# A new start and new step orders for a gated linear kernel with Strassen-type products on one Trainium2 core

## What is computed

```python
xn = (x - mean(x)) / sqrt(var(x) + 1e-5)          # x: 2 x 1024 rows of 1024, by row
w  = weight * (32x32 block of the mask has any 1) # 1024 x 1024
s  = xn @ w.T + bias
base  = xn @ W_org.T
q     = mean over the 1024 rows of a batch of xn, @ Wq.T
coeffs = softmax(q @ lora_keys.T / sqrt(128))     # 8 experts, one set per batch
delta = sum over e of coeffs[e] * (xn @ lora_down[e]) @ lora_up[e]
out = x + s * silu(base + delta)
```

## Time and profile before

| | |
|---|---|
| runs | 438.54, 437.90, 437.91 us; median 437.91 us |
| profiled execution: span from first to last instruction | 438.5 us (beside the slowest of the three runs, 438.54) |
| PE busy | 424.7 us, 97% |
| DVE busy | 334.7 us, 76% |
| ACT busy | 216.4 us, 49% |
| POOL busy | 104.9 us, 24% |
| chain that ended last | PE 75%, DMA 14%, DVE 4%, POOL 2% |
| mean DMA rate | 230 GB/s |

### The profile page before, as it was taken

How to read it: one execution, slowest core, us unless ns; L and a number is a source line. 1 busy time by engine, 2 the same in 40 slices (tenths; PEclk the granted TensorE clock), 3 DMA queues, 4 the chain that set the end, 5 groups by cost and what they waited for, 6 DMA issues and landing times.

```text
span 438.5 us, 5903 instructions
## 1 busy us (share of the span) xinstructions
PE 424.7 (97%) x1910; PEld 345.7 (79%) x1910; DVE 334.7 (76%) x492; ACT 216.4 (49%) x379; POOL 104.9 (24%) x91
## 2 busy tenths in 40 slices
...
GB/s 299 413 416 240 161 266 255 280 210 218 195 237 264 265 290 283 290 325 362 179 73 144 49 114 275 287 236 336 410 386 165 96 76 21 72 270 242 265 160 96
DMA packets 40862, 101.05 MB, mean 230 GB/s; under 512 B 4608, under 2 KB 4864, under 8 KB 40064
## 3 DMA queue, kind: packets, MB, share of 16 engines
...
...
HBM read 71.31 MB, written 29.36 MB: 230 GB/s over the span
## 4 chain that ended last, share of the span: by engine, by line
PE 75%; DMA 14%; DVE 4%; POOL 2%; SPq 2%; issue 1%; ACT 1%; DVEq 0%; ACTq 0%; POOLq 0%
PE psA L864 24%; PE psA L866 24%; PE psA L865 24%; DMA x_nat_sb<-in_x_nat_dram 4%; DMA d_dram<-d_split 3%; DMA a_raw<-in_up_dram 2%; DMA out_dram<-cst 2%; DMA worg_sb<-in_w_org_dram 2%; DMA b_hi<-d_dram 2%; PE psA L883 1%; DVE nat_stats L1154 1%; DMA temp<-in_down_dram 1%; SPq L796 1%; DVE cst L1323 1%; POOL x_nat_sb L1365 1%
## 5 line engine op out<-in xcount | busy, mean ns | idle before, releaser
L864 PE MATMUL psA<-b_hi,a_hi 128*128 128x512 f32 (+1 forms) x444 | 173.6, 391 | 0.5 <-ACT snaps L1107 0.5
L866 PE MATMUL psA<-b_hi,a_lo 128*128 128x512 f32 (+1 forms) x444 | 172.1, 388 | 0.0
L865 PE MATMUL psA<-b_lo,a_hi 128*128 128x512 f32 (+1 forms) x444 | 172.0, 387 | 0.0
L864 PEld LDWEIGHTS psA<-b_hi,a_hi 128*128 128x128 f32 x444 | 83.4, 188 | 18.4 <-ACT snaps L1107 0.9
L866 PEld LDWEIGHTS psA<-b_hi,a_lo 128*128 128x128 f32 x444 | 83.4, 188 | 17.1
L865 PEld LDWEIGHTS psA<-b_lo,a_hi 128*128 128x128 f32 x444 | 83.4, 188 | 16.6
L1078 ACT ACTIVATE b_hi<-b_raw 128x512 fp32r<-128x512 f32 (+2 forms) x66 | 45.3, 716 | 56.0 <-DVE b_raw L1232 36.5
L1219 DVE TENSOR_TENSOR b_lo<-b_raw,b_hi 128x512 fp32r<-128x512 f32 (+2 forms) x66 | 52.0, 814 | 8.6 <-ACT b_hi L1078 8.3
L1395 POOL TENSOR_TENSOR cst<-cst,xres 128x512 f32<-128x512 f32 x15 | 23.0, 1534 | 98.7 <-DVE cst L1323 98.7
L1107 ACT ACTIVATE snaps<-psA 128x512 f32<-128x512 f32 x39 | 23.2, 595 | 42.8 <-PE psA L866 42.6
L1219 DVE TENSOR_TENSOR a_lo<-s_raw,a_hi 128x512 fp32r<-128x512 f32 x52 | 37.4, 733 | 5.2 <-ACT a_hi L1068 5.2
...
## 6 DMA issues: line engine op xcount, KB each, us to landing
...
```

The lines of the kernel that those rows point to most:

```text
L864: nc.tensor.matmul(ps, l_hi, r_hi, start=first, stop=False, skip_group_check=True)
L865: nc.tensor.matmul(ps, l_hi, r_lo, start=False, stop=False, skip_group_check=True)
L866: return nc.tensor.matmul(ps, l_lo, r_hi, start=False, stop=over, skip_group_check=True)
```

## The change

The identity is made first on POOL and has a semaphore of its own (`pool_ident`), for which the warm-up on PE and the first reduction on DVE wait; before, they waited for all constants. The first `CP` waits for the table `sel`, and `G` for `ones`. There are 29 warm-up matmuls for 34. `LN` works on half a tile (512 columns) and `TX` waits for its own half. All five order tables are new. The products' numbering is the same, and so is the order of the products on PE.

```diff
-WARM = 34
+WARM = 29
...
-        def wait_nat(eng, t):
-
-            if (t,) in dve_ln_num:
-                eng.wait_ge(dve_ln, dve_ln_num[(t,)] + 1)
+        def wait_nat(eng, t, kh):
+
+            if (t, kh) in dve_ln_num:
+                eng.wait_ge(dve_ln, dve_ln_num[(t, kh)] + 1)
...
-            pe.wait_ge(pool_ready, 3)
+            pe.wait_ge(pool_ident, 1)
...
                     bank = take_misc(st)
+                    pe.wait_ge(pool_ready, 1)
                     pe.wait_ge(dve_bmx, cb_num[(q,)] + 1)
...
-                    wait_nat(pe, t)
+                    wait_nat(pe, t, kh)
...
-            dve.wait_ge(pool_ready, 3)
+            dve.wait_ge(pool_ident, 1)
...
-                    t = st[1]
+                    _, t, kh = st
                     dve.wait_ge(pool_rstd, rstd_num[(t,)] + 1)
-                    x = nat_tile(t)
+                    x = nat_tile(t)[:, kh * H:(kh + 1) * H]
...
+            nc.gpsimd.memset(ident[:, :], 0.0).then_inc(pool_zeroed, 1)
+            pool.wait_ge(pool_zeroed, 1)
+            nc.gpsimd.affine_select(out=ident[:, :], in_=ident[:, :], compare_op=ALU.not_equal, fill=1.0,
+                                    base=0, pattern=[[-1, P]], channel_multiplier=1).then_inc(pool_ident, 1)
             nc.gpsimd.memset(neg_half[:, :], -0.5).then_inc(pool_zeroed, 1)
-            nc.gpsimd.memset(ident[:, :], 0.0).then_inc(pool_zeroed, 1)
             nc.gpsimd.memset(sel[:, :, :], 1.0).then_inc(pool_zeroed, 1)
-            nc.gpsimd.memset(ones[:, :], 1.0).then_inc(pool_ready, 1)
```

The first line of SP's table and of PE's, as an example of the tables:

```diff
-    LX0 LM0 LW0.0 LW0.1 LX1 LM1 LY LK LM2 LW1.0 LX2 LW1.1 LX3 LW2.0 LM3 LI LW3.0 LX4 RS0 LX5 RS1 RS2 ST2 RS3 LT7
+    LX0 LM0 LW0.0 LW0.1 LX1 LM1 LX2 LW1.0 LW1.1 LM2 LW3.0 LX3 LM3 LX4 LK LI LW2.0 LX5 LY RS2 RS0 RS1 ST2 RS3 ST3 LT6
...
-    CP0 TX0.0 TX0.1 P0 K CP1 TX1.0 TX1.1 P1 TX2.0 TX2.1 P2 TX3.0 P3 TX3.1 CP2 P4 P5 CP3 P6 TX4.0 TX4.1 P7 P8 P9
+    TX0.0 CP0 TX0.1 P0 TX1.0 TX1.1 CP1 P1 TX2.0 TX2.1 P2 CP2 P3 TX3.0 TX3.1 P4 P5 K P6 CP3 TX4.0 P7 TX4.1 P8 P9 P10
```

More of the change, by code:

```diff
@@ L130 @@
-    H20 H15 H19 PB4.0 BA11 QS24 X13 PB4.1 BC9 H18 QS26 BC10 BA12 X14 D0 H25 QS28 H23 QS29 BC11 BA13 H22 BA14 X15
-    QO30 H21 PB5.0 BA15 PB5.1 H26 BC13 H27 QS33 BC12 H30 H24 H32 H29 QS35 H28 QS36 QO37 BC15 PB6.0 D1 H31 H34 BC14
-    PB6.1 H37 H36 QS40 H39 D2 H33 H35 QS42 H40 QS43 QO44 D3 H38 H44 H42 D4 H41 QS47 H45 H43 QS49 H46 D5 H47 QS50
-    H48 QO51 GE0 D6 U0.0 QS53 U0.1 D7 U0.2 QS55 U0.3 GE1 QO57 HB1.1.0 U0.7 U0.4 U0.6 HB1.1.1 HB1.1.2 HB1.1.3 U0.5
-    HB1.0.0 HB1.3.0 HB1.0.1 HB1.3.1 HB1.0.2 HB1.3.2 H51 H49 HB1.0.3 H52 H50 HB1.3.3 HB1.2.0 HB1.2.1 HB1.5.0
@@ new lines @@
+    P27 P28 P29 P30 BP14 BP15 P31 P32 P33 P34 P35 P36 P37 P38 P39 P40 P41 P42 P43 P44 P45 P46 P47 P48 G0 P49 P50 P51
+    P52 G1 P53 P54 P55 P56 P57 P58 E0.0.2 E0.1.2 E0.2.2 E0.3.2 E0.0.0 E0.0.1 E0.1.0 E0.1.1 E0.2.0 E0.2.1 E0.3.0
+    E0.3.1 E0.0.3 E0.1.3 E0.2.3 E0.3.3 P59 P60 P61 P62 P63 P64 P65 P66 P67 P68 P69 P70 P71 P72 P73 P74 P75 P76 P77
+    P78 P79 P80 P81 P82 P83 P84 P85 P86 E1.0.2 E1.1.2 E1.2.2 E1.3.2 E1.0.0 E1.0.1 E1.1.0 E1.1.1 E1.2.0 E1.2.1 E1.3.0
+    E1.3.1 E1.0.3 E1.1.3 E1.2.3 E1.3.3 P87 P88 P89 P90 P91 P92 P93 P94 P95 P96 P97 P98 P99 P100 P101 P102 P103 P104
@@ new lines @@
+    P105 P106 P107 P108 P109 P110 P111 P112 P113 P114
+    """,
+    """
+    CA0.0 TC0.0 H4 TC0.1 HB0.0.0 HB0.0.3 HB0.0.2 H6 HB0.0.1 CA1.0 CA1.1 TC1.0 TC1.1 H5 H7 HB0.1.1 CA2.0 H0 CA2.1
+    HB0.1.0 TC2.0 H2 TC2.1 CA3.0 H1 H3 TC3.0 TC3.1 HB0.7.0 H8 HB0.2.0 TC4.0 X6 BA6 H10 HB0.5.0 TC4.1 X8 H9 H11
+    HB0.4.0 TC5.0 TC5.1 X7 HB0.6.0 BA7 PB3.0 X9 BC6 BA8 X10 BC7 BA9 H12 X11 BA10 BC8 BC9 H13 X12 BA11 PB4.0 H14
+    HB0.3.0 H17 H15 X13 BA12 BC10 X14 QS24 BA13 BC11 H16 D0 H18 BA14 X15 H22 QS26 H19 H21 H20 BC12 BA15 H25 H24
```

124 lines of the change are left out of this document (60 added, 64 removed).

## The result

The changed kernel takes 459.81 us (median of four runs, 459.41 to 462.58). The kernel before, run beside it on the same chip, takes 438.23 us. The ratio is 1.048, with a 95% interval of 1.043 to 1.054: about 5% slower. I had forecast 433.5 us and a range that ended at 437.4. The profiled execution has a span of 460.6 us, against 438.5 before.

The account below looks back on a forecast made before the run. PE, busy 97% of the span, was taken as the bound. The terms summed to -4.4 us; from the profiled 438.5 us, less 0.6 for the runs' median, this gave 433.5 us, range 431.6 to 437.4.

Parts of the forecast that it names:

- P1: Second product on PE, at the start: starts at 18.15 us for 20.91, so 2.75 us sooner.
- Slow clock: During P1: 3.43 us at full clock for 4.37, so -0.94 us, between -0.94 and +0.76.
- `K`: Its 16 matmuls, now between P5 and P6, no longer lie in front of a wait: +1.79 us.
- P5 waits for `V1`: P5 on PE waits for a low part from DVE, which has no pause: +0.3 us, bounds 0 and 1.
- The wait at 42.7 us: This wait of PE goes, the fifth tile being loaded 6 us earlier in the queue: -0.56 us.
- The waits at 162, 193 and 328 us: PE's waits on a `QS` copy, a lora_down piece and a W_org tile go: -0.66, -1.06, -1.86 us.
- `D` among the copies: Four `D` steps close ahead of `QS` copies on ACT cost PE +1.0 us, between 0 and 6.8.
- More work on POOL: 14 more two-input sums on POOL, sharing SBUF with DVE: +0.3 us, between 0 and 2.
- A: Rival: the clock falls anyway around the start and the 0.94 comes back, 434.4 us, up to 435.2; chance 0.25.
- B: Rival: new waits, as many as the old 3.6 us behind 100 us; only the start won, 435.7 us; chance 0.22.
- C: Rival: four `D` hold back `QS` copies, 6.8 us in place of 1.0, so slower at 439.3 us; chance 0.08.
- The sign that I named for being wrong altogether: P1 starting behind 20 us, or PE's idle time behind 45 us over 3 us.

Follow-up runs that it names:

- r1: Changed kernel with six local swaps of step order, each at a wait of PE: 457.99 us, ratio 1.043.
- e5b: Changed kernel with the first half's `D`, `G` and `U` group steps back at their time in the kernel before: 464.84 us, ratio 1.055.
- s1: Changed text and lists up to product 8, all later steps in the order and on the engines of the kernel before: 447.15 us, ratio 1.017.
- b4: Kernel before with three loads on SP put ahead of two stores and three other loads: 437.41 us, ratio 0.9948.
- e6: Kernel before with only the 32 `D` steps early, at the changed kernel's time, some 30 us sooner: 446.72 us, ratio 1.015.
- e4: Kernel before with only the 58 sums moved as in the changed kernel (36 to POOL, 22 to DVE): 439.97 us, ratio 1.0015.
- e2: Changed kernel with the 58 moved sums back on their engine of before, within the changed order: 455.71 us, ratio 1.037.
- e7: Kernel before with all 47 sums of POOL moved to DVE at the same time in the order: 439.77 us, ratio 1.0013.
- e3: Changed kernel with all 61 sums of POOL moved to DVE at the same place in time: 448.64 us, ratio 1.022.
- m1: Kernel before with a tail of DVE steps, alone and beside POOL adds: two-input SBUF adds took 1.67 us each beside POOL for 0.62 alone.
- r2: Changed kernel with some DVE and ACT steps back in the old order in two windows, 236 to 263 and 364 to 392 us: 464.49 us, ratio 1.054.

## Why the prediction was wrong, point by point

- **P1, -2.75:** right. P1 started at 17.70 us, 3.2 us sooner.
- **Slow clock, -0.94:** nearly right. From P1's start to the next step PE took 3.53 us for 4.37. But P2 then waited 0.82 us for a weight piece masked on POOL, so that this gain was gone one product later.
- **`K`, +1.79:** right in kind. P6 lost 1.6 us against P5.
- **P5 waits for `V1`, +0.3:** no wait there. But P4 lost 1.2 us to the fourth tile's transposes, which now all stand between P3 and P4 (before, half stood ahead of P3) and wait 0.39 us; I had not counted that.
- **The wait at 42.7 us, -0.56:** wrong sign. A wait of 1.7 us for `kq` stood there: `KD`, which empties the bank, ran on DVE behind `LN4.0`, and POOL's mask step stretched that from 0.53 to 3.75 us.

```profile
34.45 3.75 DVE L1166 TENSOR_SCALAR x_nat_sb<-x_nat_sb,stat 128x512 f32<-128x512 f32 x1
...
34.26 3.65 POOL L1383 TENSOR_TENSOR temp<-temp,bmask 128x2048 f32<-128x2048 f32 x1 [0.75 <-DMA temp<-in_weight_dram]
```

  With it the start's gain of 3.2 us is a loss of 0.9 at P8. In r1, e5b and s1, which start with the same lists up to there, this wait is 0.8 us and P8 stands at +0.2, 0.0 and -0.1: nothing is left of the gain there either.
- **The waits at 162, 193 and 328 us, -0.66, -1.06, -1.86:** right in size: the table falls by 0.7, 1.3 and 1.8 us there. For the first two that is partly luck, as b4 loses them too, with no edit near them.
- **`D` among the copies, +1.0 (0 to 6.8):** mis-sized. In the old order early `D` steps cost 1.5% of the time, some 6.6 us (e6). I had taken a cycle's landing at 7.3 us at worst and 1.7 us per copy. In e6 the longest landing was 6.7 us, but two `D` stood ahead of one copy, and each waited for its own load, and a wait of this length brought the slow clock with it; I had seen neither. In the changed kernel, at P36, I had taken `VD` to follow `D` at once, and it came late on DVE, as did `N12`. e5b takes 6.2 us off at P36, but it also takes steps off DVE there.
- **More work on POOL, +0.3 (0 to 2):** this is the step that failed. I counted 14 moved steps, which is only the net number: 58 changed their engine, 36 to POOL and 22 from it. And I said of DVE that it "had PE well ahead of need elsewhere". That was read from the old order, and there it holds: the same 58 moves cost nothing that shows (e4). In the new order DVE is busy 27.2 of 28 us around P62, and they cost some 5 us (the changed kernel against e2).
- **Not in the sum at all:** the order of the steps behind the start. I treated five new lists as the old ones plus a few moves. e7 and e3 put their price at 2.0%, some 9 us, with no sum on POOL at all. And with DVE's slack gone, the sums that POOL had anyway, free before, cost some 7 us more (e2 against e3). The three together, 5, 9 and 7 us, are the 21 us by which the changed kernel is slower than the one before.

The rivals: A did not happen at the start: P1 ran at full clock. The clock fell later, behind long waits. B had the mechanism ("new waits where old ones were, by SBUF contention") but allowed 3.6 us for new waits; the rises behind P8 sum to 25.2 us, 5.7 of them at P36. Against them stand 3.9 us of old waits that went. C named copies behind `D`, which e6 shows for the old order; in the changed kernel they are at most a part of the loss. The sign that I named for being wrong altogether, PE idle for over 3 us behind 45 us, came true.

The Trainium skill (SBUF — State Buffer, "SBUF: two separate sides") states that the pair of ports is taken for a whole instruction, by DVE when it has two SBUF inputs or runs in a two-port mode. I weighed only the first kind. m1 and `LN4.0` agree: one-input steps are held up too (1.40 us each, 3.75 us), though no run shows in which mode they ran, and adds with one input from PSUM are not (0.61 us each). What decided the time was whether the blocked engine had slack.

Left open: which steps of the new order make DVE late, and whether SP's list, the order of the loads, has a share; no run changes it by itself in the changed kernel. r1 and r2 moved the waits and did not remove them, and the seam in s1 hides what the start alone would give.
